# A graph network of four attention layers and a graph convolution on one core: three moves in the order of work

## The reference, cut to what matters

```python
h = relu(layernorm(x))
cond = silu(emb(node_vec1) @ f_w1 + f_b1) @ f_w2 + f_b2      # 16 per node
for i in range(4):
    y = cond_layer_norm(h, cond, s1_w[i], ...)                # xn * (1 + scale) + bias
    q, k, v = y @ wq + bq, y @ wk + bk, y @ wv + bv
    scores = (q[src] * k[dst]).sum(-1) / sqrt(128)            # one per edge and head
    ex = exp(scores - segment_max(scores, src)[src])
    attn = ex / segment_sum(ex, src)[src]
    h = h + segment_sum(attn * v[dst], src) @ wo + bo
    h = h + relu(cond_layer_norm(h, ...) @ m_w1 + m_b1) @ m_w2 + m_b2
x = x + h
x = x + gcn(relu(gcn(relu(layernorm(x)), W1, b1)), W2, b2)    # degree-normalised segment sums
```

## Time and profile before

| | us |
|---|---|
| median of 3 runs (lowest, highest) | 1907.78 (1905.8, 1908.43) |
| profiled execution | 1907.54 |
| its span, first to last instruction | 1905.7 |
| TensorE busy in the span | 1829.2 |
| VectorE, ScalarE, GpSimd busy | 1383.8, 826.1, 455.0 |
| counting stage, TensorE busy of 188 us | 156.26 |

### The profile page before, as it was taken

One profiled execution on the slowest core, in us unless ns is written; L12 is line 12 of the kernel. 1 busy time (PEld: TensorE's weight loads), 2 busy tenths in 40 slices (PEclk: granted clock), 3 DMA queues, 4 the chain that ended last, 5 costly groups with the idle time before them and its releaser, 6 DMA issues. The chain is left out here.

```text
span 1905.7 us, 33972 instructions
## 1 busy us (share of the span) xinstructions
PE 1829.2 (96%) x11796; PEld 1572.4 (83%) x11796; DVE 1383.8 (73%) x2835; ACT 826.1 (43%) x1613; POOL 455.0 (24%) x544
## 2 busy tenths in 40 slices
PE   6898998999999999999999999999999999999998
PEld 3455887999889989998899899988998999887776
DVE  7697659888885498888854988888549888875323
ACT  1542455555542255554422554544225545446220
POOL 2000234111252241112512411125124111262000
PEclk9899999999999999999999999999999999999999
DMA  4112454110401121103011211030112110522001
GB/s 141 40 40 50 136 171 133 38 37 26 126 1 45 49 60 38 37 26 125 1 45 49 60 38 37 26 126 1 45 49 60 38 37 27 150 60 53 1 1 54
DMA packets 50752, 108.40 MB, mean 57 GB/s; under 512 B 18170, under 2 KB 18222, under 8 KB 50640
## 3 DMA queue, kind: packets, MB, share of 16 engines
q1 hardware_dynamic: 50608, 106.87, 19.2%
q0 software_dynamic: 32, 0.03, 0.0%
HBM read 83.62 MB, written 23.25 MB: 56 GB/s over the span
## 5 line engine op out<-in xcount | busy, mean ns | idle before, releaser
L869 ACT ACTIVATE PT<-ps 125x500 fp32r<-125x500 f32 (+1 forms) x480 | 214.3, 519 | 320.8 <-PE ps L1763 320.8
L1670 PE MATMUL ps<-PT,V 125*128 125x250 f32 x2400 | 313.3, 284 | 1.6 <-DVE PT L1274 1.6
L1670 PE MATMUL ps<-kT,qg 128*125 128x512 f32 (+1 forms) x1440 | 304.2, 356 | 8.2 <-DVE nmx L1258 6.9
L1670 PEld LDWEIGHTS ps<-kT,qg 128*125 128x125 f32 x1440 | 247.0, 187 | 59.6 <-issue 11.8
L1670 PEld LDWEIGHTS ps<-PT,V 125*128 125x128 f32 x2400 | 289.8, 190 | 2.9 <-DVE PT L1274 2.9
L1274 DVE TENSOR_TENSOR PT<-ps,PT 125x500 fp32r<-125x500 f32 (+1 forms) x480 | 253.0, 582 | 2.1 <-ACT PT L869 1.8
L1258 DVE CUSTOM_DVE_ANT_0 SB<-ps,bt 125x1250 f32<-125x1250 f32 x140 | 203.9, 1457 | 46.7 <-PE ps L1670 44.4
L1763 PE MATMUL ps<-ident,pbuf 125*125 125x125 f32 x1600 | 202.4, 274 | 12.7 <-DVE pbuf L1267 12.7
L1763 PEld LDWEIGHTS ps<-ident,pbuf 125*125 125x125 f32 x1600 | 187.2, 189 | 15.7 <-DVE pbuf L1267 15.0
L863 ACT ACTIVATE pbuf<-SB,nmx 125x1250 f32<-125x1250 f32 x140 | 188.1, 1344 | 12.6 <-DVE nmx L1258 11.1
L1267 DVE TENSOR_SCALAR pbuf<-pbuf,rden 125x1250 f32<-125x1250 f32 x160 | 151.2, 945 | 5.6
(11 more groups left out here) (243 smaller groups left out, 2819.0 us busy)
## 6 DMA issues: line engine op xcount, KB each, us to landing
bt<-edge_bias_scratch SPq DMA_DIRECT2D x40, 546.9 KB
q_scratch<-qc SPq DMA_DIRECT2D x16, 500.0 KB, 2.6
qc<-q_scratch SPq DMA_DIRECT2D x16, 500.0 KB, 4.8
counts_scratch<-cblk SPq DMA_DIRECT2D x10, 546.9 KB
c_rows<-counts_scratch SPq DMA_DIRECT2D x10, 546.9 KB
edge_bias_scratch<-b_rows SPq DMA_DIRECT2D x10, 546.9 KB
counts<-counts_scratch SPq DMA_DIRECT2D x10, 546.9 KB
wm<-in_L_gnn_wo_dram SPq DMA_DIRECT2D x4, 1024.0 KB, 8.7
```

Of the source, the lines that this page charges most:

```text
L869: sc.activation(PT[:, h % 2, 0, a:b, u * T:(u + 1) * T], ps_T[0:T, i, 0:(b - a) * T].rearrange("p (t n) -> p t n", n=T), ACT.Copy).then_in ...
L1670: e = mm(out_, lhs(a), rhs(b), start=start and i == 0, stop=stop and i == 2)
```

## The change

Three moves. In counting, the mean comes after tile 3's one-hots instead of tile 2's, the squares after tiles 4 and 5 instead of 3 and 4, and the standard deviation at tile 6 instead of 5. In the first layer, of the two bias tiles that were made between one chunk's keys and the next chunk, one stays there and one goes between the next chunk's norm and its queries; on VectorE the matching subtraction goes behind the modulation of the norm, and the one of tile 8 ahead of the last chunk's values. In each layer's start of attention, the scores of unit 1 are written to the banks 3 to 5 (columns 1536 on) directly behind those of unit 0, ahead of `nodes(1)`; their maximum reads them there, both maxima stand ahead of both normalisations, the two exponentials stand ahead of the first `turn_out`, and the first turn, which writes the same banks, waits for the second maximum.

```diff
@@ counting: ScalarE, then VectorE
-                if t == 5:
+                if t == 6:
                     sc.preload_act_table_set("natural_log_exp_and_others")
                     node_rsqrt()
...
-                elif t <= 4:
-                    node_squares(range(5 * t - 15, 5 * t - 10))
+                elif t in (4, 5):
+                    node_squares(range(5 * t - 20, 5 * t - 15))
...
-                if t == 2:
+                if t == 3:
                     node_mean()
                 if t in (4, 5, 6):
                     split_wa_lo(6 - t)
                 if t == 5:
+                    first_ln_low()
+                if t == 6:
                     node_rstd()
-                    first_ln_low()
@@ first layer: SyncE, ScalarE, VectorE
-                        for t in (2 * i, 2 * i + 1):
+                        for t in (range(2 * i - 1, 2 * i + 1) if i else (0,)):
                             bias_row(t)
                 sp.wait_ge(s["q_mm"], KD * NC * (l + 1))
                 if first:
+                    bias_row(2 * NC - 3)
...
                     rsqrt0(f + n + 1)
+                    if first and n:
+                        bias_halves(2 * n - 1)
                     q_out(l, n)
                     k_out(l, n)
                     if first:
-                        for i in (2 * n, 2 * n + 1):
-                            bias_halves(i)
+                        bias_halves(2 * n)
                 yT_out(f + NC - 1, yTb)
+                if first:
+                    bias_halves(2 * NC - 3)
...
                 front_mod(f)
+                if first and n:
+                    edge_bias(2 * n - 1)
                 k_out(l, n)
...
                     if first:
-                        for i in (2 * n, 2 * n + 1):
-                            edge_bias(i)
+                        edge_bias(2 * n)
+                if first:
+                    edge_bias(2 * NC - 3)
                 k_out(l, NC - 1)
+                if first:
+                    edge_bias(NT - 2)
@@ start of attention: VectorE
                 v_out(l, NC - 1, 0)
                 score_max(l * NC, U, 0, True, False)
+                score_max(l * NC, U + 1, 1, True, False, ps_S2)
+                normalise(U, 0)
+                normalise(U + 1, 1)
                 v_out(l, NC - 1, 1)
-                if first:
-                    edge_bias(NT - 2)
-                normalise(U, 0)
-                score_max(l * NC, U + 1, 1, True, False)
                 if first:
                     edge_bias(NT - 1)
                 turn_low(U, 0, 0)
-                normalise(U + 1, 1)
+                dve.wait_ge(s["vt"], AHEAD + 2 * NC * (l + 1))
                 score_max(l * NC, U + 2, 0)
@@ start of attention: ScalarE
                 exp_unit(U, 0, False)
+                exp_unit(U + 1, 1, False)
                 turn_out(U, 0, 0)
-                exp_unit(U + 1, 1, False)
@@ start of attention: TensorE
                     scores(l * NC, UNITS * NC * l, 0, 0)
+                    second_scores(l * NC)
                 nodes(1, x_, WV).then_inc(s["v_mm"], 1)
-                if n == NC - 1:
-                    scores(l * NC, UNITS * NC * l + 1, 0, 1)
...
+            def second_scores(G):
+                for a, b in COLS:
+                    e = product(psf[0:T, 1536 + a:1536 + b], lambda i: qg[:, i, 0, T:2 * T], lambda i: kT[:, i, 0, a:b], True, True)
+                e.then_inc(s["S"], 1)
...
-            def turn_probs(U, u):
+            def turn_probs(U, u, first=False):
+                if first:
+                    pe.wait_ge(s["ttr"], AHEAD + U + 2)
                 pe.wait_ge(s["P"], U + 1)
...
-                    turn_probs(UNITS * NC * l + k, k)
+                    turn_probs(UNITS * NC * l + k, k, k == 0)
```

More of the change, by code:

```diff
@@ L259, in build @@
         ps_S = psf[0:T, 0:N]
+        ps_S2 = psf[0:T, 1536:1536 + N]
         ps_sb = ps[0:T, 0:4, :].rearrange("p (u a) n -> p u a n", u=2)
@@ L1248, in v_out, with score_max @@
                 v.tensor_tensor(ztmp[:, u, :], ps_q[0:T, u, :], bvb[:, :], ALU.add).then_inc(s["vt"], 1)
-            def score_max(G, U, u, first=False, own=True):
+            def score_max(G, U, u, first=False, own=True, banks=ps_S):
                 dve.wait_ge(s["S"], U + 1)
@@ L1257, in score_max @@
                 settled(dve)
-                v.tensor_tensor_reduce(out=SB[:, :] if own else P[:, u, :], in0=ps_S, in1=bt[:, u, :], scale=-1.0, scalar=FLOOR,
+                v.tensor_tensor_reduce(out=SB[:, :] if own else P[:, u, :], in0=banks, in1=bt[:, u, :], scale=-1.0, scalar=FLOOR,
                                        op0=ALU.add, op1=ALU.min, accum_out=nmx[:, u:u + 1]).then_inc(s["ttr"], 1)
@@ L1390, in degrees, with project @@
                 dve.wait_ge(s["g_dg"], 7)
-            def project(l, n):
+            def project(l, n, first):
                 f, c = 2 * NC * l + n + 1, PROJECTED[n + 1]
@@ L1407, in layer @@
                 for n in range(NC - 1):
-                    project(l, n)
+                    project(l, n, first)
                     if last and n == 1:
```

## The result

| | before | after |
|---|---|---|
| median of 5 runs (lowest, highest), us | 1906.27 (1905.51, 1908.43) | 1887.4 (1886.18, 1888.87) |
| profiled execution, us | 1907.54 | 1887.38 |
| its span | 1905.7 | 1885.5 |

The ratio is 0.99 with a 95% interval of 0.9888 to 0.9913: 18.9 us less by the medians, 20.2 between the two profiled executions. The forecast was 15.0 less.

The account below looks back on a forecast made before the run. TensorE, busy 1829.2 of 1905.7 us, was taken as the bound, so only its pauses and lower clock pay. 7.9 - 1.7 + 4.2 + 4.2 + 0.4 = 15.0 us off 1907.5 gave 1892.5, range 1887.5 to 1898.5.

Parts of the forecast that it names:

- Means a tile later: Counting, tile 3: removing TensorE's 5.57 us pause and 2.36 us of lower clock gains 7.9 us, at least 5.6.
- Squares and standard deviation: Counting: 1.6 us gained at tile 6, 2.1 pause and 1.2 clock lost at tile 7; -1.7 us together.
- the first line's 2.36: Counting, tile 3: extra time of its 54 matmuls at the lower clock, 13.51 against 11.15 us, expected to vanish.
- this one's -1.24: Counting, tile 7: clock loss charged behind the new 2.1 us pause, 1.24 us, with bounds 0 and 2.36.
- Bias rows: First layer's projection: one row at a time removes four TensorE pauses before the queries, gaining 4.2 us (2 to 4.3).
- a cost put at nothing: First layer's attention start: the two bias tiles were expected to land within 0.5 us of where they did.
- Attention, layers 2 to 4: Attention start: second scores directly behind the first gain 1.4 us per layer, 4.2 for three; bounds -0.3 to 1.9 each.
- Attention, first layer: Attention start: gain 0.4 us with the clock falling again, 1.9 without the fall, lower bound -1.5.
- Rival A: Clock keeps up at tile 7 and the first layer's start: 1.2 + 1.5 us better, 1889.8; chance 0.17.
- B: Attention's start gives nothing, as the second maximum only moves the pause: 4.6 us less gain, 1897.1; chance 0.12.
- C: Counting: another wait takes the mean's place and 7.9 us shrinks to 1 or so: 1899.4; chance 0.07.
- D: Slower: the clock falls at each attention start and stays at half, costing 37 us: 1934; chance 0.04.

Follow-up runs that it names:

- e2: Kernel after with the counting order of before put back (mean, squares, standard deviation a tile earlier); 1895.32 us.
- e5: Kernel after with node_rstd ahead of tile 7 placed before the weight split instead of between it and the LayerNorm split; 1882.19 us, ratio 0.9875 to the kernel before.
- e8: Probe: kernel after plus four unused VectorE reductions per chunk in the projection of layers 2 to 4; 1898.51 us.
- e6: e5 plus, ahead of tile 8, VectorE's low half of the condition moved behind the LayerNorm split; 1879.97 us, ratio 0.986 to the kernel before.
- e1: The kernel after run again unchanged, as reference for the kernels with one part undone; 1888.44 us, ratio 0.9902 to the kernel before.
- e3: Kernel after with two bias rows together again between keys and next chunk, only tile 8's subtraction staying ahead of the last values; 1892.48 us.
- e7: e6 plus the last bias row's subtraction placed behind the low halves of the transposed probabilities at the first layer's attention start; 1880.2 us.

## Why the prediction came near and still missed low

**Means a tile later (7.9): right.** 5.57 of pause and 2.35 of clock are gone (13.51 to 11.16); tile 3 was said to begin at 65.1 and began at 64.91. Undoing it brought both back.

**Squares and standard deviation (−1.7): mechanism right, the clock term mis-sized both ways.** The new pause was to be 2.1 and is 2.07 in all five executions with this order. Its clock loss was to be 1.24; it was 2.6, 2.5 and 2.4 in three and 0.1 in two (13.74, 13.63, 13.57, 11.23, 11.23, against 11.16). In these two, tile 8 lost 2.4 and 2.6 (15.42 and 15.58 against 13.01), in the three it lost 1.4. The pause that went at tile 6 had cost 1.68 in the profile of before and 3.04 in the one with counting undone. The stage in total: 188.34 and 189.44 in the old order, 181.03 to 183.24, mean 182.0, in five of the new: 6.9 less for 6.2 forecast. That these lie so near each other is in part luck: of the first line's 2.36 and this one's -1.24 a net gain of 1.1 was to come from the clock, and in the two compared profiles none did. I had read from one row each that 1.60 keeps the clock and 2.45 loses it; the rows of other executions show no such border.

**Bias rows (4.2): the price of a pause failed, in size, and a cost put at nothing hid it.** Each pause was priced at the idle shown, about 1.05; a chunk became 1.46 shorter. The whole projection takes 94.68 and 95.27 in the old order and 88.3 to 89.9 in eight executions of the new, 6.0 less, outside my bound of 4.3. Some 1.0 is given back where the bias tile lands later against the scores. I had said that it would land within 0.5 us of where it did, meaning relative to this work; that held in the profile of after, and not in most others. The load of the tiles was issued up to 1.2 us later against the scores. Undone as a part it was worth 4.0 by the medians: two errors of opposite sign, 1.8 too little for the pauses and nothing for the tiles, left the part near its forecast, which is luck.

**Attention, layers 2 to 4 (1.4 each): right.** 1.6 in the second and third layer. The pauses were to be 0.3 and 0.4 and are 0.19 and 0.66. The last layer can't be read from one pair (3.5), as the stage holds the clock's chance as well: 330.98 with attention undone, 332.5 with it done and counting undone. With the convolution added it is 479.6 and 478.2 in the old order and 475.9 to 478.2 in the new.

**Attention, first layer (0.4): the term that was furthest off for its size.** I took the clock to fall behind the second pause, as in the earlier trace rows. It did not in the profile of after, and the layer is 2.4 shorter there, where I gave 1.9 for the case without a fall. Over all executions it is 2.0 us shorter (383.39 and 384.02 to a mean of 381.7). Here too the fall is a matter of the execution: with the new order it came behind 2.55 (e2), 2.52 (e5), 2.14 (e8), 1.84 (e6) and 1.93 (e1), and did not come in the profile of after (1.74 and 2.04), in e3 (1.12 and 2.04) and in e7 (2.44). The kernel after shows both sides by itself. Its second profiled execution:

```profile
281.03 1.33 PE L1780 MATMUL ps<-ident,pbuf 125*125 125x125 f32 x10 [2.85 <-issue]
286.01 1.77 PE L1780 MATMUL ps<-ident,pbuf 125*125 125x125 f32 x10 [1.93 <-DVE PT L1279]
287.44 3.20 PE L1680 MATMUL ps<-kT,qg 128*125 128x512 f32 x9
```

The longest pause of all, 2.85, brought no fall, the 1.93 behind it did, and the layer took 383.65: no gain at all over the 383.39 of before. So the clock is only part of the miss. With a fall in both orders the layer took 383.65, 381.38, 381.58 and 381.89 against 383.39 and 384.02, 1.6 less by the means where the forecast had 0.4. The three shorter ones had the fall at the first turn or a tile that landed early (e6); how much belongs to each is not shown.

**The sum.** By undoing the parts, counting was worth 6.9 for 6.2 forecast, the bias rows 4.0 for 4.2 and attention 6.1 for 4.6. So what the total lacks lies mostly in attention, with the first layer's clock term as its largest piece; the mis-priced pauses are the larger error by themselves, but most of it is paid back. With 1.5 of uncertainty in each part this division is likely, not shown.

**The range.** Rival A, the clock keeping up at both places, was 1889.8. Only with the cost of a pause beyond the idle shown, 1.6 us for four, does one come to 1888. The measured 1887.4 and 1888.44 lie on either side of the range's end, so whether it held was chance; that the forecast sat 4 to 5 us too high was not. The range ended at 1887.5 because I had taken 4.3 for the most that the bias rows could give, which the nearest rows could have told me was too little: a chunk in the second layer of the kernel before has 18.53 us from queries to queries and in the first 19.99. The rivals B, C and D showed nowhere.

**What is faster than both.** e6, the kernel after with two orders changed on VectorE in counting, takes 1879.97 us: 7.4 less than the kernel after's 1887.4 of the first comparison, 25.7 less than the kernel before beside it.

## What to carry to other kernels

Price a pause by the period of the work around it, with and without the pause, not by the idle time shown. Put an instruction that is long and needs nothing new directly ahead of a place where an engine's sequencer reads values, and the chain of short dependent ones in front of that; moving the chain to another place with short work behind it only moves the pause. And where one execution shows a lower clock behind a pause, take a second execution before pricing it.

## What the hardware showed that I had not expected

- Whether the granted clock falls behind a pause differs between executions of the same instructions: 2.07 us before tile 7 with a fall in three of five, 1.6 us before tile 6 in one of two, and 2.85 us at the first turn of e1 without one. The Trainium skill (TensorE: Matmul & The Clock Gate, section "What's actually happening") says of a kernel's start that the number of matmuls at the low clock changes from run to run; these rows show the like behind pauses in the middle.
- Where the clock falls at the first turn of an attention start, the second turn's pause is nearly gone (2.55 then 0.35 in e2; 2.52 then 0.44 in e5; 2.14 then 0.27 in e8), where e1 without that fall had 2.85 then 1.93. VectorE works on meanwhile, so part of the loss is hidden.
- The clock also fell for about 1.5 us of lost time in a stretch in which TensorE had no pause but did matmuls of nine columns (0.92 and 0.91 from 1730 to 1750 in e7).
